# Three gather passes of a graph-attention kernel: rows gathered by tile into a ring of 16, then copied to their steps by SP

## The reference

```
def gatv2_layer(x, src, dst, Wl, bl, Wr, br, att, bias):
    xl = x @ Wl + bl
    xr = x @ Wr + br
    xj = xl[src]
    e = leaky_relu(xj + xr[dst], 0.2)
    logits = e @ att
    m = segment_max(logits, dst, n)
    ex = exp(logits - m[dst])
    denom = segment_sum(ex, dst, n)
    alpha = ex / (denom[dst] + EPS)
    return segment_sum(alpha[:, None] * xj, dst, n) + bias
...
x = layernorm(x + L0(x))     # gatv2_layer twice, a ReLU between
x = layernorm(x + L1(x))     # scalar score per edge, no maximum
x = layernorm(x + L2(x))     # scalar score per edge, then a GRU cell
x = layernorm(x + L3(x))     # like gatv2_layer with 8 heads
```

## Time and profile before

| | |
|---|---|
| three runs | 12935.75, 12959.7 (median), 12971.74 us |
| profiled execution, first to last instruction | 12943.7 us |
| PE busy | 10725.3 us (83%), mean granted clock 0.775 |
| POOL busy | 9352.2 us (72%) |
| DVE, ACT busy | 7913.5 us (61%), 5610.6 us (43%) |
| transfers | 749.26 MB, mean 58 GB/s |

### The profile page before, as it was taken

One profiled execution on the slowest core, in us unless ns is written; L12 is line 12 of the kernel. 1 busy time (PEld: TensorE's weight loads), 2 busy tenths in 40 slices (PEclk: granted clock), 3 DMA queues, 4 the chain that ended last, 5 costly groups with the idle time before them and its releaser, 6 DMA issues.

```text
span 12943.7 us, 281524 instructions
## 1 busy us (share of the span) xinstructions
PE 10725.3 (83%) x62317; PEld 8649.8 (67%) x62317; DVE 7913.5 (61%) x29130; ACT 5610.6 (43%) x14105; POOL 9352.2 (72%) x8593
## 2 busy tenths in 40 slices
PE   5788887788888878888888886999999878888886
PEld 4666666666666666666666665777777656666664
DVE  7666666666666655555555555333333568888887
ACT  1555555455555553333333335344444543333334
POOL 3777777577777758888888885777777447777775
PEclk7999999899999966666666667555555688889887
DMA  3222222422222224444444445222222222222222
GB/s 96 56 55 55 55 55 55 132 65 56 56 56 56 55 42 39 39 39 39 39 39 39 38 39 131 57 56 56 56 56 56 58 65 62 62 61 63 61 61 61
DMA packets 809108, 749.26 MB, mean 58 GB/s; under 512 B 264686, under 2 KB 691175, under 8 KB 808255
## 3 DMA queue, kind: packets, MB, share of 16 engines
q0 software_dynamic: 453440, 550.05, 24.5%
q1 hardware_dynamic: 354814, 191.38, 5.7%
HBM read 548.62 MB, written 192.13 MB: 57 GB/s over the span
## 4 chain that ended last, share of the span: by engine, by line
PE 52%; issue 9%; DVE 8%; DMA 6%; POOL 2%; ACT 2%; DVEq 2%; SPq 0%; POOLq 0%; ACTq 0%
PE bank L721 13%; PE bank L705 7%; PE bank L708 6%; DMA scatter_s<-dst_side 6%; PE bank L706 5%; PE bank L1181 4%; PE bank L1187 3%; PE bank L730 3%; PE bank L690 2%; PE bank L1196 2%; POOL scatter_s L1148 2%; DVE agg L929 1%; DVE dst_side L1274 1%; DVE lrelu L884 1%; PE bank L1190 1%
## 5 line engine op out<-in xcount | busy, mean ns | idle before, releaser
L1148 POOL DMA_INDIRECT scatter_s<-dst_side x1664 | 2566.9, 1543 | 555.4 <-DMA scatter_s<-dst_side 240.1
L808 ACT ACTIVATE oh_e<-bank,weight,minus_w 128x128 f32<-128x128 f32 x4992 | 1876.2, 456 | 1465.3 <-PE bank L730 1385.3
L920 DVE SCALAR_TENSOR_TENSOR agg<-agg,rescale,bank 128x130 f32 x4992 | 1680.8, 337 | 1211.0 <-PE bank L721 958.6
L706 PE MATMUL bank<-rows,ident 128*128 128x128 f32 x9984 | 2108.6, 296 | 0.0
L672 POOL DMA_INDIRECT rows<-gather_c,edge_sb x1664 | 1631.9, 981 | 599.6 <-issue 382.3
L672 POOL DMA_INDIRECT rows<-gather_b,edge_sb x1664 | 1605.9, 965 | 608.5 <-issue 314.8
L672 POOL DMA_INDIRECT rows<-gather_a,edge_sb x1664 | 1622.8, 975 | 555.4 <-issue 315.5
L672 POOL DMA_INDIRECT rows<-gather_s,edge_sb x1664 | 1570.3, 944 | 571.3 <-issue 378.7
L721 PE MATMUL bank<-rows,oh_e 128*128 128x130 f32 x9984 | 1873.4, 343 | 54.1 <-DVE agg L920 37.1
L721 PEld LDWEIGHTS bank<-rows,oh_e 128*128 128x128 f32 x9984 | 1601.6, 242 | 268.5 <-issue 230.4
L706 PEld LDWEIGHTS bank<-rows,ident 128*128 128x128 f32 x9984 | 1695.0, 213 | 0.0
(11 more groups left out here) (345 smaller groups left out, 19310.3 us busy)
## 6 DMA issues: line engine op xcount, KB each, us to landing
rows<-gather_a,edge_sb POOLq DMA_INDIRECT x1664
rows<-gather_b,edge_sb POOLq DMA_INDIRECT x1664
scatter_s<-dst_side POOLq DMA_INDIRECT x1664, 3.4
rows<-gather_s,edge_sb POOLq DMA_INDIRECT x1664
rows<-gather_c,edge_sb POOLq DMA_INDIRECT x1664
rows<-scatter_s SPq DMA_DIRECT2D x56, 455.0 KB, 6.1
scatter_s<-zeros SPq DMA_DIRECT2D x64, 390.0 KB, 5.7
edge_sb<-edge_tab SPq DMA_DIRECT2D x520, 40.0 KB
```

The source lines that it names most:

```text
L706: e.matmul(o, ident[:, :], rows[:, it.slot(), g, 0:P], start=False, stop=True).then_inc(L.side.sem, 1)
L808: e.activation(oh_e[:, g % 8, :], bank[7][:, (g % CH) * P:(g % CH + 1) * P], ACT.Relu, bias=weight[:, it.slot(2, 2), g:g + 1], scale=minus ...
L920: e.scalar_tensor_tensor(old, old, rescale[:, it.slot(2, 2), g:g + 1], sum_bank(g)[:, (g % 2) * AW:(g % 2) * AW + L.aw], ALU.mult, ALU.add ...
L1148: e.indirect_dma_start(scatter_s[k], bass.IndirectOffsetOnAxis(ap=S_.target[:, it.slot(1), g:g + 1], axis=0), S_.summed[:, g % 8, :], None ...
```

## The change

A step's rows are no longer gathered from DRAM for the step. In E0, E1 and E2 POOL gathers by tile: NGT = 98 turns of 16 tiles (1568 gathers a pass in place of 1664) into a ring of 16 places in SBUF (`tile_rows`). SP then copies, for each of the 1664 steps, the tile's 128 rows from its place in the ring to `rows[:, slot, g]`, SBUF to SBUF, from an address that is loaded into a register. E3 is left as it was.

- `pool_staged` takes the place of `pool_edges`. For each chunk of four tiles it waits until the chunk two before has landed, and until `side` of every step that reads the tiles now in those four places is done; the counts for that (4 a turn) come from a new table `tile_tab` by one register load a turn (L739). The wait for each single gather is gone.
- `sp_staged` takes the place of `sp_edges`. For each group it loads 16 places and 2 x 4 landing counts into registers (three loads, L739). For each chunk it waits for the block sums of the group four before and for the tiles to have landed, and issues four copies (L778). Behind chunk 1 of group i it issues the tables of group i+1 (L753 to L756), for which it waits for `acc` of group i-3, and the tile columns of turn i+2 (L762).
- `side` on PE waits for the chunk's copies, in E2 too.
- `row_tab1` grows by 24 columns. The preparation makes the numbers: more transfers and waits for SP, one more transpose a tile for PE, three copies a tile for ACT, some dozen small operations for DVE.
- The ring lies where `xw` and the row ring lay; the loops of SP and POOL are unrolled by 8 turns.

```diff
@@ class Edges
+                self.staged = staged is not None
+                self.rw = R8 if heads > 1 else RS if self.staged else R1
+                self.row_ring = row_sb8 if heads > 1 else row_sb1
+                if self.staged:
+                    self.fetched = staged
+                    self.cols = counts.landing("tile_columns_in", U, 1, NG)
+                    self.gat = [counts.landing(name, 2, CH, NG) for name in ("residual_saved", "table_saved", "nodes_in", "step_rows_saved")]
...
+            def landed(self, it, c, lag=0):
+                if it.j is None and it.n < lag:
+                    return None
+                sem, base = self.fetched[c % 2]
+                return sem, (it.number() - lag) * (8 * NCH * CH) + 16 * CH * (c // 2 + 1) + base
...
+        def sp_staged(e, L):
+            w = On(e, anchor)
+            ring = tile_rows(L.width)
+            def tables(it, lag):
+                u, i = it.slot(lag), it.number() - lag
+                w.hold_ge(L.acc.at(it, G - 1, lag=U + lag))
+                w.hold_ge(L.tab.at(it, lag=U + lag))
...
+            def columns(it, lag):
+                for c in (NCH - 2, NCH - 1):
+                    w.hold_ge(L.landed(it, c, lag=2 * U + lag))
+                w.hold_ge(L.cols.at(it, lag=U + lag))
+                e.dma_start(tile_sb[:, it.slot(lag, 2 * U), :], tile_tab[bass.ds(it.number() - lag, 1), :, :].rearrange("o p k -> (o p) k")
+                            ).then_inc(L.cols.sem(it, lag), 16)
+            def turn(it):
+                u = it.slot()
+                w.hold_ge(L.tab.at(it))
+                row = L.row_ring[0:1, u, R1:RS].bitcast(I32)
+                place = step_values(e, mybir.EngineType.SP, row[:, 0:G], 0, G - 1)
+                even = step_values(e, mybir.EngineType.SP, row[:, G:G + NCH], 0, FETCHED)
+                odd = step_values(e, mybir.EngineType.SP, row[:, G + NCH:], 0, FETCHED)
+                (sem0, base0), (sem1, base1) = L.fetched
+                for c in range(NCH):
+                    w.hold_ge(L.block.at(it, c, lag=U))
+                    w.hold_ge((sem0, (even[c] & 0x7fff) + base0))
+                    w.hold_ge((sem1, (odd[c] & 0x7fff) + base1))
+                    for g in range(c * CH, (c + 1) * CH):
+                        e.dma_start(rows[:, u, g, 0:L.width], ring[:, bass.ds(place[g], 1), :].rearrange("p o f -> p (o f)")
+                                    ).then_inc(L.gat[c].sem(it), 16)
+                    if c == 1:
+                        if it.runs(-1, NG):
+                            tables(it, -1)
+                        if it.runs(-2, NG):
+                            columns(it, -2)
...
+        def pool_staged(e, L):
+            w = On(e, anchor)
+            ring = tile_rows(L.width)
+            w.wait_ge(L.opened.at(0))
+            def turn(it):
+                u, first = it.slot(0, 2 * U), it.j is None and it.n == 0
+                w.hold_ge(L.cols.at(it))
+                if not first:
+                    done = step_values(e, mybir.EngineType.Pool, tile_sb[0:1, u, G:TC], 1, S + NB)
+                for c in range(NCH):
+                    w.hold_ge(L.landed(it, c - 2) if c >= 2 else L.landed(it, c + 2, lag=1))
+                    if not first:
+                        w.hold_ge((L.side.sem, (done[c] & 0x7fff) + L.side.base))
+                    for g in range(c * CH, (c + 1) * CH):
+                        e.indirect_dma_start(ring[:, g, :], None, L.src_rows,
+                                             bass.IndirectOffsetOnAxis(ap=tile_sb[:, u, g:g + 1], axis=0)
+                                             ).then_inc(L.fetched[c % 2][0], 16)
...
             def side(it, c, at):
                 w.wait_ge(L.onehot_t.at(it, c))
+                if L.vector or L.staged:
+                    w.wait_ge(L.gat[c].at(it))
                 if L.vector:
-                    w.wait_ge(L.gat[c].at(it))
                     w.wait_ge(L.larger.at(it, c - 2) if c >= 2 else L.larger.at(it, c + 2, lag=1))
```

More of the change, by code:

```diff
@@ L145, in hold_ge, with turns @@
                 self.eng.sem_inc(self.anchor, 1)
-def turns(eng, n, depth, turn, ahead=0):
+def turns(eng, n, depth, turn, ahead=0, per=U):
     assert ahead <= U
-    end = n - U if ahead else n
+    end = (n - U if ahead else n) // per * per
     for i in range(PEEL):
         turn(Turn(i))
-    with eng.Fori(PEEL // U, end // U) as j:
-        for u in range(U):
-            turn(Turn(u, j))
+    with eng.Fori(PEEL // per, end // per) as j:
+        for u in range(per):
+            turn(Turn(u, j, per))
     for i in range(end, n + depth):
@@ new lines, in step_values @@
+        def step_values(e, engine, ap, low, high):
+            _, v = nc.values_load_multi_w_load_instructions(
+                ap, engines=[engine], min_val=low, max_val=high,
+                skip_runtime_bounds_check_because="the preparation makes these numbers from the tiles' places, within these bounds")
+            return v
+        def sp_staged(e, L):
[5 more added lines that the diff above has]
+                w.hold_ge(L.tab.at(it, lag=U + lag))
+                sem = L.tab.sem(it, lag)
+                e.dma_start(edge_sb[:, u, :], edge_tab[bass.ds(i, 1), :, :].rearrange("o p k -> (o p) k")).then_inc(sem, 16)
+                e.dma_start(oh_rows[0:3, u, :], onehot_tab[:, bass.ds(i * (G * P), G * P)]).then_inc(sem, 16)
+                e.dma_start(L.row_ring[0:1, u, 0:L.rw], L.row_tab[bass.ds(i, 1), :]).then_inc(sem, 16)
+                e.dma_start(step_sb[0:G, u, 0:L.SW], step_tab[bass.ds(i * G, G), 0:L.SW]).then_inc(sem, 16)
+            def columns(it, lag):
[24 more added lines that the diff above has]
+                            columns(it, -2)
@@ L658, in turn @@
                                     ).then_inc(L.zeroed, 16)
-            turns(e, NG, 0, turn)
+            tables(Turn(0), 0)
+            columns(Turn(0), 0)
+            columns(Turn(0), -1)
+            turns(e, NG, 0, turn, ahead=2, per=2 * U)
+        def pool_staged(e, L):
[15 more added lines that the diff above has]
+                                             ).then_inc(L.fetched[c % 2][0], 16)
+            turns(e, NGT, 0, turn, per=2 * U)
         def pool_edges(e, L):
```

148 lines of the change are left out of this document (115 added, 33 removed).

## The result

The changed kernel takes 13544.67 us (median of 4 runs, 13540.37 to 13550.14). The kernel before, run beside it, takes 12962.05 us (12935.75 to 12971.74). The ratio is 1.0452, 95% interval 1.0438 to 1.0467: slower by 583 us. Forecast were 12840 us, and a range that ends at 13050.

What follows compares the result with a forecast made beforehand. POOL's gathers were taken to bound E0 and E1, PE to bound E2. E0 -98, E1 -43, E2 +10 and preparation +10 sum to -121 us from 12959.7, hence 12840 us; range 12715 to 13050.

Steps and rivals of the forecast that it cites:

- E0: Pass bound by POOL's gathers: -123 for gathers removed, +10 wait for `acc`, +10 POOL's register load, +5 later start: -98 us.
- E1: Pass bound by POOL's gathers: -98 us for the same terms, +55 for transfers of zeros: -43 us.
- E2: Pass bound by PE: nothing gained from POOL, +10 us for the start and the top of the group.
- SP keeps up, with little to spare: SP in the changed passes: its work for a group takes 17.6 us, within POOL's new pace of 19.3.
- 16 copies: SP's SBUF-to-SBUF copies in a group: 0.55 to 0.60 us each, taken as 0.57, so 9.1 us.
- three register loads: SP's loads in each group, one of 16 registers and two of four: 1.1 to 3.3 us, taken as 2.5.
- the third rival: SP becomes the bound, slower than before, from 0.75 us a copy; at 0.85 about +570 us, 13530 us; chance 0.18.
- the signs named for being wrong: Copies over 0.75 us apart, POOL idle times that PE releases, or a higher granted PE clock in E2.
- The wait for `acc`: On SP ahead of the tables and chunk 2's copies: half a microsecond late, 10 us a pass, between 0 and 52.
- the 3 us of the ring: Spare time in the loop through the tile ring: 10.8 us needed, the tile's successor wanted after 13.9 us.
- The zeroing: In E1, SP's transfers of zeros delay the next group's copies: eight turns at 7 us, 55 us.
- What gathers save: On POOL, 96 fewer gathers a pass at 1.28 us: 123 us each in E0 and E1, nothing in E2.

Runs made afterwards that it cites:

- tables_late: `aligned_2` with the next group's tables and the tile columns issued behind chunk 2 of a group, not chunk 1: 13050.72 us, ratio 1.0082 to the kernel before.
- aligned_2: The changed kernel with three unused words added per `row_tab1` row, so SP's, PE's and DVE's register loads start at multiples of 16 bytes: 13125.14 us, ratio 1.0129.
- act_tables: `aligned_2` with E2 gathering by step as before the change, and ACT issuing the four tables instead of SP in E0 and E1: 12922.33 us, ratio 0.9970.

## Why the prediction was wrong

**Where it failed.** The step is "Together 17.6 us of 19.3: SP keeps up, with little to spare". SP needed 22.0. By its terms, in E0 of the changed kernel:

| us a group | forecast | measured | measured from |
|---|---|---|---|
| 16 copies | 9.1 | 10.3 | 0.64 apart |
| tables and columns | 2.45 | 2.8 | 1412.35 to 1415.12 |
| three register loads | 2.5 | 4.6 | mean of 104 groups: 78 at 5.45, 26 at 2.09 |
| arithmetic, waits, loop | 3.5 | 4.3 | the rest of 22.0 |

The loads are the largest miss, 2.1 of 4.4 us. Even the upper bound, 3.3 us, was too low, since it took the 1.1 us of 16 registers for a bound of any load. It is near a bound for a load that starts at 16 bytes; on SP such a load took 1.46. The row could not have told: every start in the kernel before is at 16 bytes, and its maximum, 3609 ns, is one load at 2473 us, in the stretch of the zeroing. The Trainium skill (DMA: Bandwidth & Descriptors, Latency and other measured facts) has a floor of about 600 ns for such a load; four registers took 0.30 us here, half of it, and 0.87 off 16 bytes, and the page does not tell of the start.

**The copies** were off by 0.07 us each, some 1.2 us a group. I took a price for 128 pieces between 0.36 and 0.41 from transfers out of DRAM; out of SBUF it is 0.51, with pieces of 256 bytes or 512. Their landing was right, 2.0 us. The prediction sets beside it a fit that the Trainium skill (DMA: Bandwidth & Descriptors, Anatomy of one DMA — SWDGE (gpsimd) path) gives for transfers issued by GpSimd; SP issues these, so its 2.15 us are no check of the term. The rule for the third rival, that SP becomes the bound when a copy costs 0.75 us, was worked out with all other terms held at their estimates. That is why it looked far away: with the loads as they are, SP passes 20.45 us already at (20.45 - 11.7) / 16 = 0.55 us a copy. A bound that several uncertain terms reach together has to be tested on their sum.

**The third rival** is what happened in kind: SP is the bound, and POOL shows idle time that PE releases, one of the signs named for being wrong. That its number fits (13530 us at SP's group of 22.1; measured 13545 at 22.0) is luck. It has a copy at 0.85 us, and copies are 0.64 apart; and in E2 the loss, which it also puts on SP, is for the most part PE's load.

**The wait for `acc`** was put at 10 us a pass. With all loads short its place costs 51 us in E0 (`tables_late`) and 36 in E1, the upper end of what was given (52). "Which the 3 us of the ring take up most times" did not hold; that SP's own time left no such room is my reading, and no run shows it.

**E0 without the misplaced loads** would have been +31 us (`aligned_2`) and not -98, so the sign of the forecast fails even then: `aligned_2` is slower than before by 1.3%.

**The zeroing** was right in kind and low in size: +55 us forecast. E1 less E0 is 59 us in the changed kernel, 65 in `aligned_2`, 70 in `act_tables`, but -17 in the kernel before, so the change cost E1 75 us more than E0. Eight turns of 30.6 us, from one group's copies to the next one's, in place of 22.0 make 69. Its place in the timeline of SP, against the earlier trace rows: nine transfers between chunk 3 and the next group.

```profile
2645.47 7.70 SPq L787 DMA_DIRECT2D scatter_s<-zeros  x9
2660.94 5.43 SPq L778 DMA_DIRECT2D rows<-tile_rows  x8
...
2676.02 8.12 SPq L787 DMA_DIRECT2D scatter_s<-zeros  x9
2691.53 5.42 SPq L778 DMA_DIRECT2D rows<-tile_rows  x8
```

**E2** was forecast at +10 and came at +176. The bound was right: PE is at its lower clock, 0.50, before and after. But the change also lengthened PE's own load at the top of each group, which the part-by-part list didn't have, because the diff only passes another buffer to it. With all loads short E2 is +19.

**The preparation** was forecast at +10 and took 6 more. **What gathers save** was right as a price: the gathers stayed 0.30 us apart where nothing held them. Each became 15 ns longer in E0 and 22 in E1, 24 and 34 us a pass that the sum doesn't have. The saving shows in full nowhere: E0 is 20 us under before in `tables_late` and 59 in `act_tables`, of the 123 that 96 gathers are worth.

**Open.** Why the first chip is slower, in the kernel before too, was not tested. The cause of the 14 pauses of POOL in a pass (25 us) is not known.

## What to carry to other kernels

An engine whose timeline shows only issues must be budgeted like any other, register loads, arithmetic and loop turns included, and tested on the sum of the terms' upper ends. A change of a buffer's pitch or base is an edit to every register load that reads it: keep each start at a multiple of 16 bytes, and compare the durations of the same load before and after. When a queue's engine is the bound, moving a few issues, and the waits ahead of them, to an engine with room can be worth more than making the transfers smaller: 81 us of E0 here against 19.

## What was not expected of the hardware

A register load from SBUF that starts off a multiple of 16 bytes took 3.6 to 3.9 us for 16 registers, against 1.1 (PE, DVE) to 1.46 us (SP), and 0.87 us for four, against 0.30. It held on SP, PE and DVE, on three chips, in the changed kernel and, for PE and DVE, in the kernel before. Per register that is 0.22 to 0.24 us off 16 bytes in both sizes; at 16 bytes a load of four took 0.30 us and one of 16 about four times that.

The issue of a copy from SBUF to SBUF with 128 pieces took 0.51 us with pieces of 512 bytes and with pieces of 256; table loads from DRAM with as many pieces took 0.35.

At the end of SP's loop, once for eight groups, 2.4 to 3.0 us passed between the branch and the next instruction in the changed kernel (0.22 us in the shorter loop before).
